# A GNN and mixture-of-experts kernel: first experts in groups of 128 slots with second weights held on chip, part rows gathered during routing, 32-bit count halves

## The chip, the cores and the metric

The kernel runs on one core of one Trainium2 chip. The metric is device time in microseconds (us) of one execution; lower is better. The core has TensorE (PE; its weight loads are listed apart as PEld), VectorE (DVE), ScalarE (ACT), GpSimd (POOL) and SyncE (SP), each with a program of its own, which wait for one another at semaphores. SP and POOL issue the DMAs. POOL also issues every indirect DMA, in which a column of 128 row numbers in on-chip memory picks 128 rows of a table in DRAM.

## The reference, cut to what matters

6250 nodes with 256 features, 200,000 edges sorted by target. Two rounds of a graph layer and an expert layer, each added to the rows:

```python
edge_index = jnp.stack([src, dst])
x = x + L0_gnn(layernorm(x), edge_index)          # graph attention, 8 heads
x = x + L0_ffn(layernorm(x))                      # 8 experts, the best 2 of each row, 256 -> 512 -> 256
x = x + L1_gnn(layernorm(x), edge_index)          # two normalized sums over the edges; needs the node degrees
x = x + L1_ffn(layernorm(x))                      # 8 experts, the best 1, with a capacity

# L0_ffn
top_vals, top_idx = top_k(xn @ Wr + br, 2);  w = softmax(top_vals)
for e in range(8):
    h = gelu(xn @ W1[e] + b1[e])
    y += (h @ W2[e] + b2[e]) * w_full[..., e]
```

## The kernel before

The work is done in stages, one after the other, with a barrier of all engines between two of them.

**The attention stage** (lines 1190 to 1540, names `gat_...`). The edges lie in 104 steps of 16 tiles of 128 edges. For each tile POOL issues one indirect gather (line 1262, `gat_rows`), so 1664 in all, into a ring of four steps. ACT takes the source terms out of a landed step, PE turns them, DVE makes running maxima, exponents and messages (line 1407), and PE sums the messages into windows (line 1520), which DVE adds to the rows (line 1430). Beside that, each step counts 16 sources per partition for the node degrees. The source numbers lie in DRAM as two halves (`source_halves`: number divided by 128, and the remainder), made in the stage of the edge lists (lines 690 to 693). SP loads 16 columns of both into `count_halves`. DVE compares them with a row of numbers (line 1344, two instructions per step: `count_onehot_lo`, 16 x 128 elements, and `count_onehot_hi`, 16 x 49), and PE multiplies the two (line 1525). Halves, numbers and results are bfloat16.

**The front of the experts** (lines 1585 to 1780) finishes the attention rows, normalizes them and computes the router's logits. SP also fills `moe_rows_out` in DRAM with zeros here (line 1779, 25 DMAs).

**Routing** (`route`, line 2430) is one chain on DVE: the best two experts of each row, their weights, the place of each row in its expert's groups of `TOK1` = 256 slots, and then 98 pairs of one-hot tiles (lines 2593 and 2594), which PE multiplies (line 2631) into the tables of slots. POOL does nothing in it.

**The first experts** (`experts`, line 2625) run over 56 groups of 256 slots. `staged` writes, for every engine, a loop over groups with two buffers and a lag per part. Per group SP loads both weights and both biases of the group's expert (lines 2675 to 2679, 512 KB for each weight), POOL gathers 2 x 128 rows (line 2693) and scatters 2 x 128 result rows (line 2700). PE has this order: the hidden products of the group before (line 2735; per 128 of the 512 hidden values the stationary tile is `w1s[:, b, c, f:F:FC]`, every fourth column, and 256 slots stream), two turns for the code tables (line 782), four turns of rows (line 2725), then the output products of the group before (line 2745). An f32 product of two 128-row tiles is two records in the trace, a turn is one. ACT applies the gelu (line 2761), DVE writes the turned rows (line 2777) and adds the bias (line 2788). `DenseTables` runs along in the same loop: POOL gathers 128 rows of `gnn_part_rows` per group (line 755; 62 in all, six of them in `rest_rows`), DVE subtracts a number (line 767), PE turns, ACT copies (line 796), SP stores `unit_codes` (line 740), which the stage after needs.

The later stages (lines 1840 to 2260, and `experts` again for the second experts, with 512 slots) keep their code.

## Time and profile before

| | us |
|---|---|
| three runs: median (lowest to highest) | 5124.44 (5123.76 to 5125.2) |
| the profiled execution's own time | 5124.75 |
| its span, first to last instruction | 5122.9 |
| attention stage, 194 to 2354 | 2160 |
| front, 2354 to 2454 | 100 |
| routing, 2454 to 2532 | 78 |
| first experts, 2532 to 3022 | 490 |
| the rest, to the end | 2101 |

"Busy" is the time in which an engine works at something that the profile counts; "idle before" is the time for which an engine stood still before an instruction, with what ended it. "issue" means that nothing the profile shows was waited for. [...]

### The profile page before, as it was taken

The numbers are of one execution on the slowest core, as the hardware profiler recorded it, in microseconds if no ns is written. First come the engines' busy times: TensorE is split into PE (matmuls) and PEld (weight loads), VectorE is DVE, ScalarE is ACT, GpSimd is POOL, SyncE is SP. The second block draws the span as 40 slices with busy tenths as digits, with TensorE's granted clock in tenths as the row PEclk, the third lists the DMA queues.
The fourth block names the chain that finished last, engine by engine and source line by source line (L and its number), as shares of the span: only waits on it lengthen the run. The fifth ranks groups of instructions, "written<-read, shape, count | busy, mean of one in ns | idle before, by whom it ended". The sixth has DMA issues, their size and how long they took to land. (4 is left out here: it accounts for less than half of the span.)

```text
span 5122.9 us, 87171 instructions
## 1 busy us (share of the span) xinstructions
PE 4174.7 (81%) x27202; PEld 3066.2 (60%) x27203; DVE 3459.0 (68%) x7696; ACT 1648.5 (32%) x2854; POOL 2300.1 (45%) x2330
## 2 busy tenths in 40 slices
PE   3477777777777777776699964799999999958998
PEld 2355555555555555555489953466666666557787
DVE  6366766676667667768622237899998999764444
ACT  1233333333333333333122236333333333231211
POOL 1377777777777777774155620000000000024553
PEclk9677777777777777776799986899999999958999
DMA  4766666666666666656167653454545545453432
GB/s 122 188 164 164 168 162 164 163 169 162 163 165 168 162 163 165 167 157 207 63 218 232 233 176 111 87 98 85 97 87 90 93 89 95 85 184 115 136 122 87
DMA packets 978900, 733.38 MB, mean 143 GB/s; under 512 B 735781, under 2 KB 864352, under 8 KB 976628
## 3 DMA queue, kind: packets, MB, share of 16 engines
q1 hardware_dynamic: 863047, 427.75, 32.6%
q0 software_dynamic: 109264, 296.24, 21.0%
q10 hardware_dynamic: 6364, 6.40, 0.4%
q8 instruction: 141, 2.31, 0.2%
q14 instruction: 84, 0.68, 0.0%
HBM read 485.07 MB, written 92.30 MB: 113 GB/s over the span
## 5 line engine op out<-in xcount | busy, mean ns | idle before, releaser
L1262 POOL DMA_INDIRECT gat_rows<-h_rows,gat_sources x1664 | 1621.9, 975 | 509.9 <-issue 478.8
L1520 PE MATMUL gat_sum_ps<-gat_rows,gat_onehot 128*128 128x265 f32 x3328 | 1261.7, 542 | 3.7 <-DVE gat_rows L1407 3.6
L1520 PEld LDWEIGHTS gat_sum_ps<-gat_rows,gat_onehot 128*128 128x128 f32 x3328 | 861.3, 272 | 218.2 <-DVE gat_rows L1407 4.8
L2207 ACT CAST gnn_z<-build_ps 128x392 bf16<-128x392 f32 x992 | 479.7, 485 | 749.4 <-PE build_ps L2222 749.2
L2231 PE MATMUL back_ps<-zb_pieces,gnn_z 128*128 128x384 bf16 x3038 | 634.6, 325 | 0.0
L2253 PE MATMUL front_ps<-x_res_wide,front_rows 128*128 128x448 bf16 x2604 | 618.1, 351 | 0.0
L2148 DVE TENSOR_TENSOR onehot_low<-dense_codes,dense_iota_bf 128x2048 bf16<-128x2048 bf16 x496 | 603.9, 1218 | 2.0 <-PE build_ps L2222 1.9
L2127 POOL DMA_INDIRECT front_rows<-zf_piece_rows,vrow_nodes x62 | 58.8, 948 | 1148.0 <-PE front_ps L2253 1137.9
L1407 DVE TENSOR_TENSOR gat_rows<-gat_rows,gat_numerators_ps 128x1024 f32<-128x1024 f32 x416 | 502.2, 1207 | 0.0
L2222 PEld LDWEIGHTS build_ps<-onehot_high,onehot_low 128*128 128x128 bf16 x7936 | 352.6, 98 | 184.9 <-issue 38.2
L2735 PE MATMUL moe_hidden_ps<-moe_rows_T,moe_w 128*128 128x256 f32 (+1 forms) x1408 | 450.4, 475 | 2.3 <-DMA moe_b<-in_L_ffn_b 1.5
L2761 ACT ACTIVATE moe_hidden<-moe_hidden_ps,moe_b 128x256 f32<-128x256 f32 (+1 forms) x352 | 194.0, 551 | 765.3 <-PE moe_hidden_ps L2735 765.3
L2745 PE MATMUL moe_out_ps<-moe_w,moe_hidden 128*128 128x256 f32 x1920 | 434.8, 384 | 1.1 <-ACT moe_hidden L2761 1.1
L2735 PEld LDWEIGHTS moe_hidden_ps<-moe_rows_T,moe_w 128*128 128x128 f32 x1408 | 377.5, 322 | 65.3 <-issue 4.8
L2222 PE MATMUL build_ps<-onehot_high,onehot_low 128*128 128x49 bf16 x7936 | 373.5, 188 | 44.0 <-DVE onehot_high L2148 41.5
L1430 DVE TENSOR_TENSOR x_res_wide<-x_res_wide,gat_sum_ps 128x265 f32 x832 | 355.7, 428 | 66.9 <-DVE x_res_wide L1430 66.4
L2745 PEld LDWEIGHTS moe_out_ps<-moe_w,moe_hidden 128*128 128x128 f32 x1920 | 360.1, 190 | 63.0 <-issue 13.9
L2231 PEld LDWEIGHTS back_ps<-zb_pieces,gnn_z 128*128 128x128 bf16 x3038 | 263.2, 97 | 150.7 <-issue 1.3
L1280 ACT ACTIVATE gat_numerators_ps<-gat_exponents 128x128 f32<-128x128 f32 x104 | 29.3, 281 | 906.2 <-DVE gat_exponents L1400 759.4
L2160 DVE TENSOR_TENSOR gnn_z<-gnn_z,front_ps 128x448 f32<-128x448 f32 x434 | 267.8, 617 | 74.8 <-PE front_ps L2253 73.3
L1493 PE MATMUL gat_turned_ps<-ident,gat_src_terms 128*128 128x128 f32 x104 | 49.3, 474 | 324.7 <-ACT gat_src_terms L1274 324.7
L2253 PEld LDWEIGHTS front_ps<-x_res_wide,front_rows 128*128 128x128 bf16 x2604 | 222.9, 97 | 139.8 <-issue 0.3
(377 smaller groups left out, 5467.5 us busy)
## 6 DMA issues: line engine op xcount, KB each, us to landing
moe_w<-in_L_ffn_W SPq DMA_DIRECT2D x112, 512.0 KB
gat_targets<-gat_step_targets SPq DMA_DIRECT2D x104, 512.0 KB
moe_w<-in_L_ffn_w SPq DMA_DIRECT2D x32, 1024.0 KB
gat_rows<-h_rows,gat_sources POOLq DMA_INDIRECT x1664
gat_flags<-gat_tile_flags SPq DMA_DIRECT2D x104, 128.0 KB
normal_rows<-moe_xn_all SPq DMA_DIRECT2D x14, 896.0 KB
mid_taken<-moe_rows_out SPq DMA_DIRECT2D x14, 896.0 KB, 7.4
moe_rows_out<-slot_zeros SPq DMA_DIRECT2D x24, 512.0 KB
```

The source lines that it names most:

```text
L1262: pool.indirect_dma_start(out=g[:, b, t, :], out_offset=None, in_=T.h[:, :], in_offset=bass.IndirectOffsetOnAxis(ap=idx[:, b, t:t + 1], ax ...
L1407: dve.tensor_tensor(rows[:, :, :, 0:HD], rows[:, :, :, 0:HD], pW[:, n * PART:(n + 1) * PART, :].unsqueeze(3).to_broadcast([P, PART, H, HD] ...
L1430: dve.tensor_tensor(window(w), window(w), po[:, s % BANKS, 0:W], ALU.add).then_inc(ad, 1)
L1520: last = pe.matmul(po[:, s % BANKS, 0:W], o[:, b, s * SUB + t, :], g[:, b, s * SUB + t, :], start=t == 0, stop=t == SUB - 1)
L2148: last = dve.tensor_tensor(out[:, n, :, :, :], ct[:, k % SLOTS, a, at].rearrange("p (u t) -> p u t", t=HITS).unsqueeze(2) .to_broadcast(sh ...
L2160: dve.tensor_tensor(yfT[:, at:at + CN], yfT[:, at:at + CN], pf[:, n, 0:CN], ALU.add).then_inc(ya, 1)
L2207: nc.scalar.copy(AT[:, k % 2, :, CHUNK * c:CHUNK * (c + 1)], pb[:, c % 2, 0:CHUNK * NT].rearrange("p (u h) -> p h u", u=CHUNK)).then_inc(a ...
L2222: last = pe.matmul(pb[:, c % 2, u * NT:(u + 1) * NT], ol[:, n, i, :, t], oj[:, n, i, :, t], start=True, stop=True)
L2231: ins = pe.matmul(py[:, (k - 1) % 2, 0:3 * P], AT[:, (k - 1) % 2, h, :], zb3[:, h, :, :].rearrange("p s f -> p (s f)"), start=h == 0, stop ...
L2253: ins = pe.matmul(pf[:, bank, 0:CN], zfv[:, first + s, m * P:(m + 1) * P], AV[:, first + s, chunk * CN:(chunk + 1) * CN], start=n == 0, st ...
L2735: last = pe.matmul(ph[:, f % 2, 0:tok], w1s[:, b, c, f:F:FC], xT[:, b, c, :], start=c == 0, stop=c == 1)
L2745: last = pe.matmul(py[:, q % 2, 0:D], hT[:, f, q * P:(q + 1) * P], w2s[:, b, f, :], start=f == 0, stop=f == FC - 1)
```

## The change

1. `TOK1` goes from 256 to 128: 106 groups of 128 slots in place of 56 of 256.
2. `resident_experts` takes the place of `experts` for the first experts. The second weights, their biases and the first biases of all eight experts lie in on-chip memory for the whole stage (`Resident`); they are loaded in the front, behind the loads of the rows, and a group loads its first weights alone. Each engine that needs the expert's number reads four numbers from a table every two groups (`Choice.fetch`). The hidden units of a product are now 128 neighbouring columns of the first weights (`f * P:(f + 1) * P`). Hidden values have two buffers, their PSUM tile four, and the output products come two groups behind. `phased` writes the loops, without the part for the code tables once its 62 turns are done.
3. All 62 gathers of part rows are issued by POOL during routing (`gather_parts`); in the experts DVE writes a bfloat16 copy (two instructions), which PE turns.
4. `src_hi`, `src_lo`, `src_void`, `source_halves` and `count_halves` become f32. The numbers they are compared with and the one-hots stay bfloat16.
5. Only the pad rows of `moe_rows_out` are zeroed.

```diff
-TOK1 = 256
+TOK1 = 128
...
-        hi = k.sb(ctx, "src_hi", [P, BG * BLK], BF16)
-        lo = k.sb(ctx, "src_lo", [P, BG * BLK], BF16)
+        hi = k.sb(ctx, "src_hi", [P, BG * BLK])
+        lo = k.sb(ctx, "src_lo", [P, BG * BLK])
...
+def gather_parts(pool, S, C, T, parts, sem):
+
+    for s in range(S.SUPER):
+        pool.indirect_dma_start(
+            out=parts[:, s, :, :].rearrange("p a e -> p (a e)"), out_offset=None, in_=T.gnn[:, :],
+            in_offset=bass.IndirectOffsetOnAxis(ap=C.vpart[:, s:s + 1], axis=0)).then_inc(sem, 16)
...
-        hl = k.sb(ctx, "count_halves", [P, RING, 2, CH], BF16)
+        hl = k.sb(ctx, "count_halves", [P, RING, 2, CH])
...
-        self.filled = zero_fill(sp, [self.y1[0:2 * self.S.ROWS, :], *self.more], self.zf, self.zs)
+        pads = self.S.ROWS - self.S.N
+        for a in range(2):
+            sp.dma_start(self.y1[a * self.S.ROWS + self.S.N:(a + 1) * self.S.ROWS, :], self.zf[0:pads, :]).then_inc(self.zs, 16)
+        self.filled = 32
+        self.weights.load(sp)
...
+    def load(self, sp):
+        w1, b1, w2, b2 = self.dram
+        sp.dma_start(self.b1[:, :, :], b1.rearrange("e (c p) -> p e c", p=P), allow_slow_non_contiguous=True).then_inc(self.wl, 16)
+        for e in range(self.X):
+            sp.dma_start(self.w2[:, e, :, :], w2[e].rearrange("(c p) d -> p c d", p=P)).then_inc(self.wl, 16)
...
+            def load(i, b, t, first):
+                e = sp.value_load(gtab[0:1, bass.ds(t, 1)], min_val=0, max_val=W.X - 1)
+                if not first:
+                    sp.wait_ge(hp, (t - 1) * FC)
+                    sp.nop(nofuse=True)
+                sp.dma_start(w1s[:, b, :, :], W.dram[0][bass.ds(e, 1), :, :].rearrange("a (c p) f -> p (a c) f", p=P)).then_inc(wl[b], 16)
+            phased(sp, groups, [(0, None, load), (2, S.SUPER, side.store(sp))], 2)
+            side.stored(sp)
...
+            def take(t):
+                if t >= 2:
+                    pool.wait_ge(tp, t - 1)
+                pool.indirect_dma_start(
+                    out=xr[:, t % 2, :], out_offset=None, in_=xn[:, :],
+                    in_offset=bass.IndirectOffsetOnAxis(ap=src_of[:, t:t + 1], axis=0)).then_inc(xl[t % 2], 16)
+
+            def put(t):
+                pool.wait_ge(yc, t + 1)
+                pool.indirect_dma_start(
+                    out=y[:, :], out_offset=bass.IndirectOffsetOnAxis(ap=dst_of[:, t:t + 1], axis=0),
+                    in_=yo[:, t % 2, :], in_offset=None).then_inc(ys[t % 2], 16)
+            for t in range(groups + 4):
+                if t < groups:
+                    take(t)
+                if t >= 4:
+                    put(t - 4)
...
+            def hidden(i, b, t, first):
+                pe.wait_ge(tc, t + 1)
+                pe.wait_ge(wl[b], i * 16 + 16)
+                for f in range(FC):
+                    if not (first and b == 0):
+                        pe.wait_ge(hc, t * FC + (f + 1 - FC))
+                    for c in range(2):
+                        last = pe.matmul(ph[:, f, 0:P], w1s[:, b, c, f * P:(f + 1) * P], xT[:, b, c, :],
+                                         start=c == 0, stop=c == 1)
+                    last.then_inc(hp, 1)
+
+            def outs(i, b, t, first):
+                e = expert.at(2, b)
+                pe.wait_ge(hc, t * FC + FC)
+                if not first:
+                    pe.wait_ge(yc, t - 1)
+                for f in range(FC):
+                    last = pe.matmul(py[:, b, 0:D], hT[:, b, f, :], W.w2[:, bass.ds(e, 1), f, :].rearrange("p a d -> p (a d)"),
+                                     start=f == 0, stop=f == FC - 1)
+                last.then_inc(yp, 1)
+
+            pe.wait_ge(side.ir, 1)
+            pe.wait_ge(W.wl, W.full)
+            phased(pe, groups, [(1, None, hidden), (1, S.SUPER, side.turn(pe)), (0, None, turn), (2, None, outs)], 2, expert.fetch)
...
-        T.halves = k.dram("source_halves", [P, 2, S.BATCH * CH], BF16)
+        T.halves = k.dram("source_halves", [P, 2, S.BATCH * CH])
...
+                if tables is not None:
+                    k.pg = k.sem("unit_part_rows_gathered")
+                    k.parts = k.sb(ctx, "unit_part_rows", [P, S.SUPER, 2, P])
+                route(k, S, C, tag, tok, logits, bias, choices, X, capacity, src_of, dst_of, weight, gtab, final, tables)
```

On PE, in the first experts just ahead of their loop (names as in the profile; `x8` is eight products, `ISA` works on registers), stands before, for one group of 256 slots, behind the turns and output products of the group before:

```order
L2725 MATMUL moe_turn_ps<-ident,moe_rows 128x128 x4
L2745 MATMUL moe_out_ps<-moe_w,moe_hidden 128x256 x8
L2735 MATMUL moe_hidden_ps<-moe_rows_T,moe_w 128x256 x8
L782 MATMUL codes_ps<-ident,part_rows 128x128 x2
L2725 MATMUL moe_turn_ps<-ident,moe_rows 128x128 x4
L2745 MATMUL moe_out_ps<-moe_w,moe_hidden 128x256 x8
```

and now, for one group of 128 slots (the loads of the expert's number stand before every second group):

```order
L2798 TENSOR_LOAD moe_group_expert
L2890 MATMUL moe_hidden_ps<-moe_rows_T,moe_w 128x128 x8
L771 MATMUL codes_ps<-codes_ident,part_codes 128x128 x2
L2880 MATMUL moe_turn_ps<-ident,moe_rows 128x128 x2
L2900 ISA
L2900 MATMUL moe_out_ps<-moe_w,moe_hidden 128x256
L2900 ISA
L2900 MATMUL moe_out_ps<-moe_w,moe_hidden 128x256
L2900 ISA
L2900 MATMUL moe_out_ps<-moe_w,moe_hidden 128x256
L2900 ISA
L2900 MATMUL moe_out_ps<-moe_w,moe_hidden 128x256
```

Eight hidden products stream 128 columns where eight streamed 256, four output products take the place of eight, and a register instruction stands before each of them.

On POOL, at the start of the experts and in routing, before:

```order
L2693 DMA moe_rows<-normal_rows,moe_slot_source 128x256 x4
L755 DMA part_rows<-gnn_part_rows,vrow_part 128x256
L2693 DMA moe_rows<-normal_rows,moe_slot_source 128x256 x2
L755 DMA part_rows<-gnn_part_rows,vrow_part 128x256
L755 DMA rest_rows<-gnn_part_rows,vrow_part 128x256 x6
L2700 DMA moe_rows_out<-moe_out_rows,moe_slot_target 26880x256 x2
```

and now (the first row opens routing, the two branches behind the 62 gathers are its closing barrier):

```order
L2601 UNCONDITIONAL_BRANCH
L718 DMA unit_part_rows<-gnn_part_rows,vrow_part 128x256 x62
L2435 UNCONDITIONAL_BRANCH
L2849 UNCONDITIONAL_BRANCH
L2854 DMA moe_rows<-normal_rows,moe_slot_source 128x256 x5
```

The gathers of part rows have left the loop of the experts and stand between two barriers with routing's DVE chain.

## Rows read from the trace of the kernel before

**Rows 1.** Stages: us, busy of PE, PEld, DVE, ACT, POOL, clock, DMA, GB/s.

```profile
194.00:2354.00 2160.00, 1647.72 (x8006) 1186.72 (x8007) 1496.49 (x3851) 704.81 (x729) 1621.94 (x1664) 0.75 0.61 162
2354.00:2454.00 100.00, 64.48 (x298) 58.12 (x296) 75.50 (x174) 46.53 (x155) 39.26 (x9) 0.53 0.68 257
2454.00:2532.00 78.00, 46.55 (x200) 31.47 (x200) 70.73 (x275) 1.53 (x2) 0.00 (x0) 0.76 0.00 1
2532.00:3022.00 490.00, 466.64 (x2140) 422.81 (x2140) 121.25 (x286) 124.96 (x287) 278.04 (x286) 0.97 0.67 220
```

**Rows 2.** Groups by line, attention stage: count, busy, mean ns, idle before.

```profile
L1262 POOL DMA_INDIRECT gat_rows<-h_rows,gat_sources x1664 | 1621.9, 975 | 509.9 <-issue 478.8 <-PE gat_sum_ps L1520 27.7 <-DMA gat_sources<-step_sources 3.4
```

**Rows 3.** Waits in the attention stage: total, times, longest.

```profile
DVE gat_running L1353 <- PE gat_turned_ps L1493: 356.2, 104, 12.6
```

**Rows 4.** Timeline of POOL, one step: start, us, instruction.

```profile
1500.47 1.04 POOL L1262 DMA_INDIRECT gat_rows<-h_rows,gat_sources  x1 [0.30 <-issue]
...
1503.06 1.73 POOL L1262 DMA_INDIRECT gat_rows<-h_rows,gat_sources  x1 [0.30 <-issue]
1505.09 0.95 POOL L1262 DMA_INDIRECT gat_rows<-h_rows,gat_sources  x1 [0.30 <-issue]
```

**Rows 5.** Timeline of DVE, the same stretch.

```profile
1500.40 0.29 DVE L1399 TENSOR_TENSOR gat_exponents<-gat_sums 128x128 f32<-128x128 f32 x1
...
1502.74 1.23 DVE L1344 TENSOR_TENSOR count_onehot_lo<-count_halves,count_iota 128x2048 bf16<-128x2048 bf16 x1 [0.99 <-PE gat_sum_ps L1520]
1503.89 0.56 DVE L1344 TENSOR_TENSOR count_onehot_hi<-count_halves,count_iota 128x784 bf16<-128x784 bf16 x1
1507.79 0.42 DVE L1353 TENSOR_TENSOR_SCAN gat_running<-gat_flags,gat_turned_ps 128x128 f32<-128x128 f32 x1 [3.34 <-PE gat_turned_ps L1493]
```

**Rows 6.** Line 1262: ns min/median/max.

```profile
L1262 POOL DMA_INDIRECT gat_rows<-h_rows,gat_sources x1664: 942/946/1925, 195.0 to 2322.3; - x185
```

**Rows 7.** Line 1344.

```profile
L1344 DVE TENSOR_TENSOR count_onehot_lo<-count_halves,count_iota x104: 1224/1226/1227, 228.2 to 2342.7; 128x2048 bf16<-128x2048 bf16 x104
L1344 DVE TENSOR_TENSOR count_onehot_hi<-count_halves,count_iota x104: 557/559/562, 229.3 to 2343.8; 128x784 bf16<-128x784 bf16 x104
```

**Rows 8.** Line 1407, f32 with f32.

```profile
L1407 DVE TENSOR_TENSOR gat_rows<-gat_rows,gat_numerators_ps x416: 1186/1214/1219, 240.2 to 2351.0; 128x1024 f32<-128x1024 f32 x139
```

**Rows 9.** Line 1970, f32 with bfloat16 (`zf_pieces`).

```profile
L1970 DVE TENSOR_TENSOR mid_rest<-gnn_z,zf_pieces x7: 1080/1085/1087, 3066.6 to 3203.2; 128x896 f32<-128x896 f32 x7
```

**Rows 10.** Timeline of PE, one group of the first experts.

```profile
2701.11 4.07 PE L2735 MATMUL moe_hidden_ps<-moe_rows_T,moe_w 128*128 128x256 f32 x16
2705.01 0.38 PE L782 MATMUL codes_ps<-ident,part_rows 128*128 128x128 f32 x2
2705.23 0.60 PE L2725 MATMUL moe_turn_ps<-ident,moe_rows 128*128 128x128 f32 x4
2705.81 3.71 PE L2745 MATMUL moe_out_ps<-moe_w,moe_hidden 128*128 128x256 f32 x16
2709.37 2.88 PE L2735 MATMUL moe_hidden_ps<-moe_rows_T,moe_w 128*128 128x256 f32 x11
```

**Rows 11.** Timeline of the weight loads, first experts.

```profile
2705.12 0.47 PEld L2725 LDWEIGHTS moe_turn_ps<-ident,moe_rows 128*128 128x128 f32 x4
```

**Rows 12.** The same in the front, clock 0.53.

```profile
2445.30 0.93 PEld L1768 LDWEIGHTS moe_po<-w_router,moe_xT 128*128 128x128 f32 x4 [0.87 <-ACT moe_xT L1728]
```

**Rows 13.** DMA issues, first experts: KB each, median us to landing.

```profile
unit_codes<-codes_out SPq DMA_DIRECT2D x49, 64.0 KB, 4.8
```

**Rows 14.** The page, DMA issues.

```profile
mid_taken<-moe_rows_out SPq DMA_DIRECT2D x14, 896.0 KB, 7.4
```

**Rows 15.** DVE, first and last of routing.

```profile
2454.16 0.57 DVE L2498 TENSOR_TENSOR moe_logits<-moe_raw_logits,b_router 128x392 f32<-128x392 f32 x1 [17.00 <-PEq L1658]
...
2531.43 0.22 DVE L2606 TENSOR_SCALAR moe_slot_source<-moe_slot_token 128x112 int32<-128x112 f32 x1
```

**Rows 16.** Groups by line in routing.

```profile
L2594 DVE TENSOR_SCALAR moe_onehot_tile<-iota,moe_slot_tile,moe_token_number 128x112 f32<-128x112 f32 x98 | 33.8, 345 | 0.0
```

288 lines of the change are left out of this document (179 added, 109 removed).

## The prediction

> **What bounds the kernel now.** I read the table of stages first, then in each stage that the change touches who is busy and who waits. Attention takes 2160 us of the span [rows 1]. POOL is busy for 1621.9 us of it in 1664 indirect gathers; of the 509.9 us between them 478.8 are "issue", 0.30 us behind each, and only 27.7 are put down to a buffer that PE frees [rows 2]. 1621.9 + 509.9 = 2132 us, the stage but for its ends: attention is a row of gathers on POOL, 16 x (0.946 + 0.306) = 20.0 us per step at the median gather [rows 6], and 20.5 us by the sums. DVE is busy for 1496 of 2160 us and waits in each step for PE, 356.2 us / 104 = 3.4 us at line 1353 alone [rows 1, 3]. Routing is 78 us in which DVE works and POOL does nothing [rows 1]. In the first experts PE is busy for 467 of 490 us at clock 0.97 [rows 1]: PE sets the pace, 8.26 us per group (2701.11 to 2709.37) [rows 10].
>
> **The 32-bit halves (part 4) are the largest term.** First the duration. With everything bfloat16 a one-hot of 2048 elements takes 1.226 us and one of 784 takes 0.559 us [rows 7]. An f32 sum of 1024 elements takes 1.214 us [rows 8], so f32 goes at half the pace of bfloat16. What counts is one f32 input beside a bfloat16 one, and that form is in the trace: 896 elements in 1.085 us [rows 9]. From 896 to 1024 elements the time grows by 0.129 us, 1.01 ns per element. So 2048 elements come to 1.214 + 1024 x 1.01 = 2.25 us (plus 1.02) and 784 to 0.97 us (plus 0.41). DVE gets 1.43 us per step more, which its 3.4 us of waiting behind these two instructions [rows 3, 5] can hold.
>
> [...]
>
> Then what it does to POOL. One gather per step is stretched: that of 1503.06 takes 1.73 us where the median is 0.946 [rows 4, 6]. It begins while `count_onehot_lo` (1502.74 to 1503.97) runs [rows 5] and ends 0.82 us behind that instruction's end. The gather of 1500.47 takes 1.04 us beside an f32 instruction with two inputs in on-chip memory (line 1399) that ends at 1500.69, and ends 0.82 us behind it as well [rows 4, 5]. So a gather wants something about 0.13 us after its start (0.946 - 0.82), and stands still until such a DVE instruction, bfloat16 or f32, is over. Over the stage the stretch is 1621.9 - 1664 x 0.946 = 47.8 us, 0.46 us per step, nearly all from `count_onehot_lo` [rows 2, 6, 7].
>
> Gathers begin every 1.25 us, so an instruction of 2.25 us must catch one. If it starts at the same phase as now, the caught gather waits for as much longer as the instruction is longer: 1.02 us. Behind it POOL's next gather asks 0.82 + 0.30 + 0.13 = 1.25 us after the end of the first one-hot, when the second (0.97 us) is over, as now. 104 x 1.02 = **106 us**, on POOL's path, which sets the end of the stage. Bounds: at the most favourable phase the wait is 2.25 - 1.25 = 1.0 us, 0.54 more than now: 56 us; at the worst it is 2.25 us: 186 us. I take the equal phase, since the start of the one-hot hangs on PE's sums of gathered rows and those on the same gathers.
>
> [...]
>
> The wider stores of the edge lists and loads of 64 instead of 32 bytes a row lie beside DVE's and POOL's work: 1 us (0 to 4).
>
> **Routing (part 3).** 62 gathers at 0.946 + 0.306 take 77.6 us [rows 2, 6], and the DVE chain beside them 2454.16 to 2531.65, 77.5 us [rows 15]: two equal paths, both ahead of a barrier. DVE's instructions are of the kind that made gathers wait: most read on-chip memory twice, or are one-hots of 0.29 to 0.35 us back to back [rows 16]. A wait of half such an instruction, about 0.13 us, at each gather gives 62 x 0.13 = **+8 us**. Bounds: 0, if they never meet; 62 x 0.35 = 22 us. DVE itself isn't slowed: `count_onehot_lo` takes 1224 to 1227 ns whether or not a gather runs [rows 7]. The slightly wider group tables cost under 1 us. What leaves the experts' loop there was hidden under PE and gives nothing.
>
> **The first experts (parts 1 and 2).** Now, per group of 256 slots [rows 10]: hidden products 3.90 us for 16 records (0.244 each), code turns 0.22 for 2, row turns 4 x 0.11 + 0.14, output products 16 x 0.213 + 0.15. The output products, whose stationary columns are neighbours, are at the pace of their 256 columns; the hidden ones, with every fourth column, are slower by 0.03 us each.
>
> After it, per group of 128: 16 hidden records of 128 columns, 8 output records of 256, 2 row turns, and for 62 groups 2 bfloat16 turns. What 128 f32 columns cost is in the row turns: their 4 weight loads pass in 0.47 us, under 0.12 us each [rows 11]. The loads ahead of the router's products say it at the lower clock: 4 in 0.93 us, at most 0.23 us each, at a granted clock of 0.53 [rows 1, 12]. So loads keep up with 128 columns, which stream in half of 0.213 us: 16 x 0.107 = 1.71, output 8 x 0.213 + 0.15 = 1.86, row turns 0.22 + 0.14, code turns about 0.12 (0.10 to 0.22): 4.05 us, or 3.93 without code turns.
>
> Then the loads. The first weights of group t are asked for when the hidden products of t - 2 are done and needed two group times later, less these products. Their landing isn't listed; 64 KB take 4.8 us from issue and 896 KB 7.4 us [rows 13, 14], by interpolation 512 KB take 6.2 us. Two groups can't be faster than 1.71 + 0.2 + 6.2 = 8.1 us: 4.06 per group, level with PE. I take 4.1. POOL's one gather and one scatter per group are 2 x 1.25 = 2.5 us, under it. The DMAs move 512 + 128 + 128 + 64 KB in 4.1 us, 208 GB/s, against 220 now [rows 1]. The reads of the expert's number fall under the 1.7 us of queued output products. 106 x 4.1 = 435 us against 56 x 8.26 = 463: **-28 us**. Bounds: PE alone, 424 (-39); weights late with 7.4 us, 4.5 per group, 477 (+14). At the start DVE now waits for 1 MB of second biases and for the last part rows before it copies a turned row; PE's first hidden products and all behind them wait for that: +2 us (0 to 6).
>
> The zero fill and the load of the second weights lie in the front, where the chain over PE, ACT and DVE sets the end at 0.68 DMA share [rows 1]: 0.
>
> **Sum.** 106 + 1 + 8 - 28 + 2 = 89 us on the profiled execution's 5124.75 (span 5122.9 and 1.85 around it), which is 0.3 above the median: **5214 us**.
>
> **Rivals.**
> A, the forecast: the longer one-hot holds up one gather per step. For it: rows 4, 5 and 9. 5214, own range 5165 to 5275. 75%.
> B, the other side: the one-hots cost POOL nothing more. Either the form with f32 halves keeps its 1.23 us, or DVE comes to them at a time when the stretch stays 0.46 us per step. Then attention stays at 2160 us and the rest is -17: 5108, faster. It decides as soon as attention grows by less than 17 us, 0.16 us per step. Against it: rows 9, and gathers every 1.25 us. 13%.
> C, DVE's chain takes the whole 1.43 us per step into the step time, because the numerators come late and with them the free buffers: 149 us, 5257. For it: POOL shows 27.7 us under "PE `gat_sum_ps`" [rows 2]; against it: the 3.4 us of slack. 7%.
> D, the experts are bound by the landing of the first weights with A holding, or the change in routing slows DVE too: 5214 + 42 + 14 = 5270. 5%.
>
> **Numbers.** A measurement of this kernel tells about 0.2%, 10 us, from no change. Faster by that: B, 13%, and a hair of A: 0.14. The same: 0.04. Slower: 0.82. The range of 8 in 10 leaves out the lower half of B and the upper end of C and D: 5110 to 5270; the likeliest case's own is 5165 to 5275.
>
> **What would show it.** Right: `count_onehot_lo` at 2.2 to 2.3 us, `count_onehot_hi` near 0.97; gathers of line 1262 at a mean of about 1.04 us, one per step near 2.4 us; attention at about 2266 us; POOL the last to end routing at 86 us; a group of the experts at 4.1 us with hidden products 0.107 us apart. Wrong: one-hots at 1.23 us, or attention under 2180 us; hidden products 0.19 us apart, which would make the experts slower than before by 60 us and more.

## The result, and the profile after

| | us |
|---|---|
| before, in the comparison (4 runs) | 5124.82 (5123.76 to 5125.97) |
| after (4 runs) | 5163.66 (5161.9 to 5165.16) |
| ratio, 95% interval | 1.0076 (1.0058 to 1.0093) |
| forecast | 5214 (5110 to 5270) |

Slower, as forecast, but by 39 us and not by 89. The spans of the two profiled executions differ by 38.6 us (5122.9, 5161.5), and divide so, each stage from its first instruction to that of the next:

| stage | before | after | change | forecast |
|---|---|---|---|---|
| up to the end of attention | 2357.0 | 2452.3 | +95.3 | +107 |
| front | 97.2 | 97.1 | -0.1 | 0 |
| routing | 78.6 | 87.0 | +8.4 | +8 |
| first experts | 491.3 | 430.0 | **-61.3** | -26 |
| the rest | 2098.8 | 2095.1 | -3.7 | 0 |

The stages of the kernel after (the columns are those of [rows 1]):

```profile
194.00:2452.00 2258.00, 1625.68 (x8009) 1148.27 (x8009) 1650.68 (x3854) 704.67 (x729) 1713.38 (x1664) 0.76 0.59 156
2452.00:2549.40 97.40, 63.67 (x294) 57.76 (x294) 74.24 (x172) 46.59 (x156) 38.65 (x9) 0.52 0.57 176
2549.40:2636.30 86.90, 45.76 (x200) 32.25 (x200) 72.39 (x275) 1.48 (x2) 61.77 (x62) 0.76 0.30 94
2636.30:3066.40 430.10, 408.91 (x2880) 380.58 (x2880) 143.19 (x443) 174.25 (x489) 206.12 (x212) 0.98 0.64 206
```

**Attention.** The gathers, whose line is now 1243, against [rows 2]; then the two one-hots against [rows 7] (ns min/median/max):

```profile
L1243 POOL DMA_INDIRECT gat_rows<-h_rows,gat_sources x1664 | 1713.4, 1030 | 510.0 <-issue 479.5 <-PE gat_sum_ps L1501 27.1 <-DMA gat_sources<-step_sources 3.4
```

```profile
L1325 DVE TENSOR_TENSOR count_onehot_lo<-count_halves,count_iota x104: 2291/2293/2366, 228.5 to 2434.7; 128x2048 bf16<-128x2048 f32 x104
L1325 DVE TENSOR_TENSOR count_onehot_hi<-count_halves,count_iota x104: 959/968/971, 230.7 to 2437.0; 128x784 bf16<-128x784 f32 x104
```

POOL is busy for 91.5 us more, and its idle time behind the gathers is the same (510.0 against 509.9). So 1.030 against 0.975 us per gather makes 91.5 of the 95 us. Some 3 more lie behind the last gather, in a tail of 36.3 us against 33.3, with a mean granted clock (TensorE's, as a share of its full speed) of 0.74 against 0.90. One caught gather, on POOL and beside it on DVE:

```profile
1515.78 0.95 POOL L1243 DMA_INDIRECT gat_rows<-h_rows,gat_sources  x1 [0.30 <-issue]
1517.03 2.50 POOL L1243 DMA_INDIRECT gat_rows<-h_rows,gat_sources  x1 [0.30 <-issue]
1519.84 0.94 POOL L1243 DMA_INDIRECT gat_rows<-h_rows,gat_sources  x1 [0.30 <-issue]
```

```profile
1516.43 2.29 DVE L1325 TENSOR_TENSOR count_onehot_lo<-count_halves,count_iota 128x2048 bf16<-128x2048 f32 x1 [0.51 <-PE gat_sum_ps L1501]
1518.64 0.97 DVE L1325 TENSOR_TENSOR count_onehot_hi<-count_halves,count_iota 128x784 bf16<-128x784 f32 x1
```

The gather begins in the one-hot, which ends at 1518.72, and ends at 1519.53, 0.81 us behind it: the pattern of [rows 4, 5] with a longer instruction. It takes 1.55 us longer than the median.

**Routing.** The part gathers (min/median/max), the last of them, the first gather of the experts, and the end of DVE's chain:

```profile
L718 POOL DMA_INDIRECT unit_part_rows<-gnn_part_rows,vrow_part x62: 942/1015/1161, 2550.0 to 2629.4; - x62
```

```profile
2629.41 0.95 POOL L718 DMA_INDIRECT unit_part_rows<-gnn_part_rows,vrow_part  x1 [0.31 <-issue]
2636.36 0.94 POOL L2854 DMA_INDIRECT moe_rows<-normal_rows,moe_slot_source  x1 [6.01 <-POOLq L2435]
```

```profile
2628.32 0.22 DVE L2591 TENSOR_SCALAR moe_slot_source<-moe_slot_token 128x106 int32<-128x106 f32 x1
```

POOL's last gather ends 1.8 us behind DVE's chain, and POOL goes on 6.01 us after it. In the kernel before POOL went on 1.15 us behind DVE's last instruction (2531.65 [rows 15], first gather at 2532.80). DVE's chain itself, 2549.39 to 2628.54, is 1.7 us longer than it was, but it no longer ends last.

**The first experts.** PE in one group of 128 slots without code turns (rows are listed as in [rows 10]; a run of records ends later than the next begins, so starts are compared):

```profile
2950.43 1.95 PE L2890 MATMUL moe_hidden_ps<-moe_rows_T,moe_w 128*128 128x128 f32 x16
2952.22 0.38 PE L2880 MATMUL moe_turn_ps<-ident,moe_rows 128*128 128x128 f32 x2
2952.44 1.89 PE L2900 MATMUL moe_out_ps<-moe_w,moe_hidden 128*128 x8
2954.16 0.27 PE L2890 MATMUL moe_hidden_ps<-moe_rows_T,moe_w 128*128 128x128 f32 x1
```

1.79 + 0.22 + 1.72 = 3.73 us, with nothing between the parts. With code turns it is 3.85, and every fourth of those groups 4.13; the mean over the 105 steps from row turn to row turn (2641.90 to 3045.51) is 3.84.

### The profile page after: what moved, and what is told of

It is laid out like the page before. It is cut to its first block and busy times, and to the rows that moved or that the text cites. A ratio compares the mean times of both kernels' runs of the same rounds, so it can differ in the third digit from the quotient of the medians.

```text
span 5161.5 us, 90934 instructions
## 1 busy us (share of the span) xinstructions
PE 4091.3 (79%) x27942; PEld 2985.3 (58%) x27943; DVE 3637.5 (70%) x7853; ACT 1696.7 (33%) x3055; POOL 2380.6 (46%) x2318
## 5 line engine op out<-in xcount | busy, mean ns | idle before, releaser
L1243 POOL DMA_INDIRECT gat_rows<-h_rows,gat_sources x1664 | 1713.4, 1030 | 510.0 <-issue 479.5
L1501 PE MATMUL gat_sum_ps<-gat_rows,gat_onehot 128*128 128x265 f32 x3328 | 1181.5, 514 | 1.7 <-DVE gat_rows L1388 1.6
L1501 PEld LDWEIGHTS gat_sum_ps<-gat_rows,gat_onehot 128*128 128x128 f32 x3328 | 797.1, 252 | 189.9 <-DVE gat_rows L1388 2.3
L1334 DVE TENSOR_TENSOR_SCAN gat_running<-gat_flags,gat_turned_ps 128x128 f32<-128x128 f32 x104 | 43.8, 421 | 345.0 <-PE gat_turned_ps L1474 345.0
L1325 DVE TENSOR_TENSOR count_onehot_lo<-count_halves,count_iota 128x2048 bf16<-128x2048 f32 x104 | 238.9, 2297 | 64.1 <-PE gat_sum_ps L1501 52.3
L2133 DVE TENSOR_TENSOR onehot_high<-dense_codes,dense_iota_bf 128x784 bf16<-128x784 bf16 x496 | 279.0, 562 | 0.0
L1255 ACT COPY gat_src_terms<-gat_rows 128x128 f32<-128x128 f32 x104 | 43.4, 418 | 662.7 <-DMA gat_rows<-h_rows,gat_sources 662.7
L1474 PEld LDWEIGHTS gat_turned_ps<-ident,gat_src_terms 128*128 128x128 f32 x104 | 18.9, 182 | 398.4 <-ACT gat_src_terms L1255 398.4
```

The costliest lines, as they stand in the source:

```text
L1243: pool.indirect_dma_start(out=g[:, b, t, :], out_offset=None, in_=T.h[:, :], in_offset=bass.IndirectOffsetOnAxis(ap=idx[:, b, t:t + 1], ax ...
L1325: last = dve.tensor_tensor(out[:, :, :, :], hl[:, b, half, :].rearrange("p (u t) -> p u t", t=2).unsqueeze(2).to_broadcast(shape), iob[:, ...
L1501: last = pe.matmul(po[:, s % BANKS, 0:W], o[:, b, s * SUB + t, :], g[:, b, s * SUB + t, :], start=t == 0, stop=t == SUB - 1)
L2133: last = dve.tensor_tensor(out[:, n, :, :, :], ct[:, k % SLOTS, a, at].rearrange("p (u t) -> p u t", t=HITS).unsqueeze(2) .to_broadcast(sh ...
```

## The experiments

Times stand against the kernel before in the same comparison (5125.56, 5126.06, 5127.03 and 5128.07 us in the four of them). B16 is short for "the changed kernel with bfloat16 halves", the first run.

### The halves alone, taken out and put in

e1, the change without its part 4:

```diff
-        hl = k.sb(ctx, "count_halves", [P, RING, 2, CH])
+        hl = k.sb(ctx, "count_halves", [P, RING, 2, CH], BF16)
...                 # and src_hi, src_lo, src_void, source_halves likewise
```

> The changed kernel with the halves of the source numbers in bfloat16 again, all other parts kept. Theory L (the attention stage lost 94.5 us because the one-hots in f32 stand longer in the way of the gathers, and nothing else moved there): the one-hots are back at 1.226 and 0.559 us, attention is back at its length of before, and the time is 5163.7 - 94.5 = 5069 us, 55 us under the kernel before. Rival R (part of the loss comes from another part of the change, such as where buffers or transfers now lie): attention stays 20 us or more above its length of before, 5090 us and more.

Measured: 5075.35 us, ratio 0.9903 (0.9886 to 0.9919).

e2, the kernel before with that part alone (the same lines the other way round):

> The kernel before with the halves of the source numbers in f32 and nothing else changed. Theory L: attention grows by the same 94.5 us, 5124.8 + 94.5 = 5219 us, count_onehot_lo near 2.29 us, the mean gather 1.03 us. Rival R: less than 75 us, under 5200 us.

Measured: 5218.50 us, ratio 1.0182 (1.0165 to 1.0199).

Taken out of the change the halves give back 5163.7 - 5075.4 = 88 us, put into the kernel before they cost 93 us. L holds; the rest of the change by itself is worth 50 us. The gathers in e1 and e2:

```profile
L1243 POOL DMA_INDIRECT gat_rows<-h_rows,gat_sources x1664 | 1623.6, 976 | 510.2 <-issue 479.6 <-PE gat_sum_ps L1501 27.1 <-DMA gat_sources<-step_sources 3.4
```

```profile
L1262 POOL DMA_INDIRECT gat_rows<-h_rows,gat_sources x1664 | 1712.7, 1029 | 510.0 <-issue 477.6 <-PE gat_sum_ps L1520 28.9 <-DMA gat_sources<-step_sources 3.4
```

### The same work in more instructions

e3 (4 and 2 pieces, f32), e4 (2 and 1, bfloat16) and e13 (2 and 1, f32) differ in the counts and the type of the halves (the diff shows e3):

```diff
-                    shape = [P, CH // 2, w, 2]
-                    last = dve.tensor_tensor(out[:, :, :, :], ...
+                    for g in range(4 if half else 2):
+                        n = CH // 2 // (4 if half else 2)
+                        shape = [P, n, w, 2]
+                        last = dve.tensor_tensor(out[:, g * n:(g + 1) * n, :, :], ...
```

> The changed kernel (halves in f32) with the same one-hot elements written by more instructions: count_onehot_lo in 4 of 512 elements, count_onehot_hi in 2 of 392. Theory I (a gather that asks while a DVE instruction with two inputs runs waits for the end of that one instruction only, and gets in before the next): each caught gather waits 0.3 us on the mean instead of 1.2, two or three are caught per step, 0.7 to 0.9 us per step instead of 1.24: 35 to 55 us less, 5110 to 5130 us; no gather near 2.5 us is left, the longest is about 1.6. Rival T (the gather waits until DVE is through with its row of such instructions, or what counts is their sum): no gain, 5164 us or a few us more for the four added instructions, and gathers of 2.5 us and longer.

Measured: 5067.95 us, ratio 0.9889 (0.9873 to 0.9906).

> The changed kernel with bfloat16 halves and count_onehot_lo written by 2 instructions of 1024 elements. Theory I: a caught gather waits 0.3 us on the mean instead of 0.6, so 0.30 us per step instead of 0.46: 10 to 25 us less than with bfloat16 halves alone, 5044 to 5059 us; the longest gathers near 1.6 instead of 1.9 us. Rival T: no gain, 5069 to 5074 us.

Measured: 5047.77 us, ratio 0.9851 (0.9835 to 0.9867).

> The changed kernel with f32 halves (5163.7 us) and count_onehot_lo in 2 instructions of 1024 elements, count_onehot_hi in one as before. In the run with 4 and 2 pieces a gather that started within 0.1 us of a piece's start was not held up, and a gather that a piece had held up asked again just at the start of a later one. Theory I (a gather waits only for an instruction that began before it, and after a release its successor asks 1.25 us later, which here is when the next instruction, 1.19 us later, has just begun): one held gather per step, 0.6 us instead of 1.24: 5070 to 5110 us. Rival P (what made the run with 4 and 2 pieces fast is that its pieces are short, all of them are waited for): the second gather meets the second piece or the 0.97 us of count_onehot_hi, 1.1 us per step and more, 5145 us and over.

Measured: 5163.06 us, ratio 1.0069 (1.0054 to 1.0085).

e3 gained 96 us where I expected 35 to 55, e4 28, as expected, and e13 nothing at all, where theory I had it at 5070 to 5110 us. DVE's work did not shrink in e3, it grew: the one-hots of a step take 3.5 us with their six instructions and 3.2 with two. The gathers shrank, from a mean of 1030 ns to 970, and the longest from 2909 to 1467. First the lines of e3 (a group by line; ns min/median/max), then POOL and DVE in a step of e13:

```profile
L1243 POOL DMA_INDIRECT gat_rows<-h_rows,gat_sources x1664 | 1613.9, 970 | 510.0 <-issue 496.5 <-PE gat_sum_ps L1503 10.1 <-DMA gat_sources<-step_sources 3.4
```

```profile
L1327 DVE TENSOR_TENSOR count_onehot_lo<-count_halves,count_iota x416: 677/685/767, 230.3 to 2340.0; 128x512 bf16<-128x512 f32 x139
```

```profile
1515.98 1.57 POOL L1243 DMA_INDIRECT gat_rows<-h_rows,gat_sources  x1 [0.30 <-issue]
1517.85 1.71 POOL L1243 DMA_INDIRECT gat_rows<-h_rows,gat_sources  x1 [0.30 <-issue]
```

```profile
1515.50 2.36 DVE L1327 TENSOR_TENSOR count_onehot_lo<-count_halves,count_iota 128x1024 bf16<-128x1024 f32 x2 [0.51 <-issue]
1517.77 0.97 DVE L1327 TENSOR_TENSOR count_onehot_hi<-count_halves,count_iota 128x784 bf16<-128x784 f32 x1
```

The first gather is held by the first piece (1515.50 to 1516.72) and ends 0.83 us behind it, though the second piece follows at once: so far theory I. The next gather starts at 1517.85, 0.08 us after the one-hot of 784 elements, and is held to its end. That is what rival P had named as one of its two ways (the second gather meets `count_onehot_hi`), and its time was the right one. I had let a gather go free that starts up to 0.1 us behind an instruction; 0.08 was already too late.

In e3 the pieces start 0.60 us apart. The gather behind a released one starts 0.82 + 0.30 = 1.12 us behind the end of the piece that held the first, which is 1.20 us behind the start of the next piece: level with the one after that, often to 0.01 us, and it goes free. That the two periods agree was luck: the expectation had not counted on it.

So the refined rule, as the traces here show it, is: **a gather is held when it starts after a DVE instruction did that has both inputs in SBUF (the on-chip memory that is not PSUM), to that instruction's end; one that started first is not.** Of the gathers that started over 0.05 us behind the start of such an instruction and over 0.18 us ahead of its end, all were held in the 16 traces: 1464 of 1464 in the one-hots, 406 of 406 in `gat_exponents`, 370 of 370 in two forms of `gat_sums`, and they ended 0.81 to 0.83 us behind it. (Those held by the scan of line 1364, whose inputs all lie in SBUF, ended 0.75 to 0.76 us behind its end in the changed kernel.) The place of the inputs counts. In the changed kernel 349 gathers started within line 1388 (`gat_rows` times `gat_numerators_ps`, 1.21 us, two inputs, one of them in PSUM), and in the kernel before 331 within its line 1407; none of them took over 0.97 us.

How sharp "first" is, twelve of the traces tell at the one-hots. Of the gathers that started up to 0.1 us ahead of one (393) or less than 0.02 us behind its start (153) none was held; of 26 between 0.02 and 0.05 us behind it 5 were; of 142 between 0.05 and 0.1 all. Where the gather got in first at such a close start, the one-hot took up to 0.08 us longer: DVE pays that much at most, and the gather the rest of the instruction.

With the instructions' starts and lengths of each run, and gathers that may start anywhere in their 1.25 us, this rule gives 0.51 us held per step for bfloat16, 1.53 for f32, 0.44 for e3, 0.26 for e4, 1.26 for e13. The traces (busy time less 1664 times the median, over 104 steps) have 0.46, 1.34, 0.38, 0.17 and 1.27: the order is right, and the sizes to 0.2 us. The measured figures in the expectation of e15 below are up to 0.06 higher than this count gives.

### One input in place of two

e9 is B16 and, behind the one-hots:

```diff
+                dve.tensor_reduce(scr[:, :], C.iota[:, 0:P].unsqueeze(1).to_broadcast([P, 11, P]), AX.X, ALU.add)
```

> The changed kernel with bfloat16 halves (5075.4 us) and one more VectorE instruction per step behind the two one-hots: a reduction of 11 x 128 f32 numbers, which has one input, about 1.5 us long; nobody reads its result. It adds to VectorE what the change to f32 added, 1.5 us against 1.43. Theory L (what holds gathers up is a DVE instruction with two inputs, and VectorE's own time is off the path): no more than 10 us, 5065 to 5085 us, no gather longer than with bfloat16 halves alone (1.93 us). Rival C (VectorE's time is on the path, or any DVE instruction holds gathers up): 70 to 156 us more, 5145 us and over.

Measured: 5074.58 us, ratio 0.9898 (0.9883 to 0.9913). DVE's new instruction (a group by line) and the gathers:

```profile
L1330 DVE TENSOR_REDUCE spare_sum<-iota 128x11 f32<-128x1408 f32 x104 | 167.6, 1611 | 0.0
```

```profile
L1244 POOL DMA_INDIRECT gat_rows<-h_rows,gat_sources x1664 | 1622.1, 975 | 510.2 <-issue 479.4 <-PE gat_sum_ps L1503 27.4 <-DMA gat_sources<-step_sources 3.4
```

One step of it, DVE and POOL:

```profile
1259.09 1.61 DVE L1330 TENSOR_REDUCE spare_sum<-iota 128x11 f32<-128x1408 f32 x1
```

```profile
1259.82 0.94 POOL L1244 DMA_INDIRECT gat_rows<-h_rows,gat_sources  x1 [0.30 <-issue]
```

1.61 us per step on DVE cost nothing, where 1.43 us more in instructions with two inputs cost 88. Rival C of the prediction falls. And the reduction did have gathers to hold: in 102 of the 104 steps one starts within it, 0.73 us behind its start on the median, and none takes over 0.95 us. Held as the one-hots hold them, these gathers would have cost about 0.75 us each, an estimate from the rule, 77 us in all. (A twin of this instruction with two inputs in SBUF was not run.)

### The first experts

e6 is B16 with the output products one group earlier (and the expert's number taken to match):

```diff
-            phased(pe, groups, [(1, None, hidden), (1, S.SUPER, side.turn(pe)), (0, None, turn), (2, None, outs)], 2, expert.fetch)
+            phased(pe, groups, [(1, None, hidden), (1, S.SUPER, side.turn(pe)), (0, None, turn), (1, None, outs)], 2, expert.fetch)
```

> The changed kernel with bfloat16 halves (5075.4 us), in which TensorE makes the output products of a group right behind its hidden products, as the kernel before did, instead of one group later. The group of 128 slots takes 3.73 us in the changed kernel's trace without code turns and 3.85 with them; the forecast had 4.05. Theory G (the 0.29 us too much are the two pauses that I carried over from the kernel before, and the later output products are what took them away): pauses of 0.2 to 0.4 us come back ahead of the output products, 106 x 0.29 = 31 us, 5096 to 5118 us. Rival N (a group is only its streaming time, the order of the products costs nothing): 5070 to 5082 us.

Measured: 5144.99 us, ratio 1.0039 (1.0025 to 1.0053). PE in e6:

```profile
2705.66 1.95 PE L2890 MATMUL moe_hidden_ps<-moe_rows_T,moe_w 128*128 128x128 f32 x16
2707.44 0.27 PE L771 MATMUL codes_ps<-codes_ident,part_codes 128*128 128x128 bf16 x2
2707.55 0.39 PE L2880 MATMUL moe_turn_ps<-ident,moe_rows 128*128 128x128 f32 x2
2708.24 1.99 PE L2900 MATMUL moe_out_ps<-moe_w,moe_hidden 128*128 x8 [0.30 <-ACT moe_hidden L2918]
2710.57 1.60 PE L2890 MATMUL moe_hidden_ps<-moe_rows_T,moe_w 128*128 128x128 f32 x12 [0.33 <-issue]
```

The pause ahead of the output products is back (0.69 us from the row turns' start, 0.22 without it), and the first output product takes 0.10 us more. There is more than I expected: a second pause, of 0.33 us, ahead of the hidden products in every fourth group, whose cause no run shows. A group takes 4.42 us, every fourth 4.8 to 5.0. The lag is worth 70 us, 0.66 per group. Rival N falls, and theory G holds in its cause but not in its size: 70 us are twice its 31, and 5145 us lie outside its range.

e7 is B16 with the columns as before:

```diff
-                        last = pe.matmul(ph[:, f, 0:P], w1s[:, b, c, f * P:(f + 1) * P], xT[:, b, c, :],
+                        last = pe.matmul(ph[:, f, 0:P], w1s[:, b, c, f:F:FC], xT[:, b, c, :],
```

> The changed kernel with bfloat16 halves (5075.4 us), with the first weights loaded into TensorE by every fourth column as in the kernel before (and the rows of the second weights and the first biases in the order that goes with it). Theory L (such a load lasts 0.244 us, which in the kernel before just topped the 0.213 us in which 256 columns stream, and 128 columns take 0.112): hidden products 0.244 us apart, 16 x 0.132 x 106 = 224 us more, near 5299 us. Rival A (it adds the same 0.031 us to each product): 16 x 0.031 x 106 = 53 us more, near 5128 us. Rival N: no difference, 5075 us.

Measured: 5262.54 us, ratio 1.0268 (1.0251 to 1.0285). PE in e7:

```profile
2703.29 3.79 PE L2890 MATMUL moe_hidden_ps<-moe_rows_T,moe_w 128*128 128x128 f32 x16
2706.91 0.28 PE L771 MATMUL codes_ps<-codes_ident,part_codes 128*128 128x128 bf16 x2
```

Products 3.62 / 16 = 0.226 us apart on the mean, where columns side by side give 0.112: 187 us, near L (224) and far from A (53). Behind the first, which follows at 0.12 us, they are 0.233 us apart. That is also their distance in the kernel before, where 256 columns stream and not 128; with the columns side by side 256 columns are 0.216 apart (e8, e16). The weight loads (PEld, 2650 to 2950 us) last 0.326 us on the mean in the kernel before and 0.328 in e7, where they last 0.19 with the columns side by side (after, e8, e16). As the distance is the same 0.233 us at both widths, I take it for the pace of the load of every fourth column: it is 0.017 us above the 0.216 of 256 columns and 0.121 above the 0.112 of 128. (The 0.244 of the prediction is the mean of 16 records with two pauses of 0.08 us among them.)

e8 and e16 put the columns side by side in the kernel before; e8 with the biases and second weights in the order that goes with them, e16 with the columns alone:

```diff
-                        last = pe.matmul(ph[:, f % 2, 0:tok], w1s[:, b, c, f:F:FC], xT[:, b, c, :],
+                        last = pe.matmul(ph[:, f % 2, 0:tok], w1s[:, b, c, f * P:(f + 1) * P], xT[:, b, c, :],
...                 # e8 only:
-                sp.dma_start(b1s[:, b, :], b1[bass.ds(e, 1), :].rearrange("a (p c) -> p (a c)", p=P)).then_inc(wl[b], 16)
+                sp.dma_start(b1s[:, b, :], b1[bass.ds(e, 1), :].rearrange("a (c p) -> p (a c)", p=P), allow_slow_non_contiguous=True).then_inc(wl[b], 16)
```

> The kernel before (5124.8 us, groups of 256 slots), with only the columns of a hidden product side by side in the first and second experts (the second weights' rows and the first biases in the order that goes with it). Theories L and A of the run e7 say the same: hidden products 0.213 us apart instead of 0.244, a group of the first experts shorter by 16 x 0.031 = 0.50 us, 56 x 0.50 = 28 us less there; the second experts, whose products have 512 columns, gain nothing if the load is what counts (L), 5097 us, and 16 x 0.031 x 16 = 8 us more if it is a fixed addition (A), 5089 us. Rival M (the transfers become the bound at 7.7 us per group, or the first biases, now read as single numbers, delay the weights): less than 12 us gained, over 5113 us.

Measured: 5122.03 us, ratio 0.9993 (0.9984 to 1.0003): no difference that can be told. PE waits for the expert's loads ten times between 2580 and 3000 us, and never in that stretch of the kernel before (in all, times, longest), in e8:

```profile
PE moe_hidden_ps L2735 <- DMA moe_b<-in_L_ffn_b: 4.7, 10, 1.2
```

> The kernel before with only the columns of a hidden product side by side in the two experts' stages; biases and second weights stay as they are, so a hidden unit gets the bias and the second weight of another and the output is not the reference's. In the run that also changed the order of the biases the shortest groups of the first experts took 7.85 us where 8.17 are usual, many up to 9 us. Theory S (7.85 is what the columns give, the longer groups came from the biases read as single numbers): steady groups of 7.85 us, 56 x 0.32 = 18 us less, 5107 us. Rival T (the transfers can't bring the weights of a group in 7.85 us): groups above 8.0 us on the mean again, less than 8 us gained, over 5117 us.

Measured: 5112.82 us, ratio 0.9970 (0.9958 to 0.9981). Groups of 7.86 us with few exceptions, where the kernel before has 8.17 and e8 anything from 7.86 to 9.4. So the columns are worth 15 us in groups of 256. The groups of the second experts, with 512 columns, gain 0.02 us of 28.6 in both runs, which is L and not A. What eats the gain in e8 is one of two things, as it differs from e16 in both: the first biases, read as single numbers (512 pieces of 4 bytes per group), or the second weights, read in rows of 1024 bytes instead of 4096. In the traces the packets of the second weights fill the same share of the DMA engines' time in both (0.19 in e8, 0.20 in e16, 2600 to 3000 us), and those of the first biases rise from 0.01 to 0.03. That speaks for the biases, but neither was run alone. The change reads both once, in the front.

e12 is the kernel before without its six part rows in one go:

```diff
-        for x in self.rest_at(t):
-            take(self.S.G1 + x, self.vx[:, x, :, :], self.xg)
...
-            for x in self.rest_at(t):
-                turned(2 + x, self.vx[:, x, :, :])
```

> The kernel before (5124.8 us) without the gather, the subtraction, the turns and the copies of the 6 part rows that it makes in one go in its second group of the first experts; their codes are stored from another row, so that part of the output is not the reference's. In the trace of before the row turns of the first groups are 14.64, 9.82 and 8.86 us apart and later ones 8.17. Theory B (TensorE waits there for one copy after the other, 6.5 us, and then runs at the lower clock for a while): 8 to 10 us less, 5115 to 5117 us, and groups of 8.2 to 9 us from the start. Rival W (the first groups are late because their weights are): 14.64 stays above 12 us and the time within 3 us of 5124.8.

Measured: 5116.13 us, ratio 0.9980 (0.9971 to 0.9990). The row turns are now 8.52, 8.02, 8.02 and 10.36 us apart. Theory B: 10 us. In the step of 10.36 PE waits for the expert's loads (0.63 us) and for ACT (0.97), which the theory had not foreseen. What goes was to be seen on PE in the kernel before, at the first groups:

```profile
2556.56 0.38 PE L782 MATMUL codes_ps<-ident,part_rows 128*128 128x128 f32 x2
2557.64 0.41 PE L782 MATMUL codes_ps<-ident,rest_rows 128*128 128x128 f32 x2 [0.70 <-ACT codes_out L796]
2558.60 0.41 PE L782 MATMUL codes_ps<-ident,rest_rows 128*128 128x128 f32 x2 [0.55 <-ACT rest_codes_out L799]
...
2563.39 1.06 PE L2725 MATMUL moe_turn_ps<-ident,moe_rows 128*128 128x128 f32 x4
2564.24 5.17 PE L2745 MATMUL moe_out_ps<-moe_w,moe_hidden 128*128 128x256 f32 x16
```

6.8 us from 2556.56 to the row turns, which other groups reach in 0.22, and then output products at a slower pace: 16 in 5.0 us to the next start, 3.56 in steady groups. The granted clock is 0.5 from 2560.6 to 2567.4, behind the pauses between the copies, and 1.0 on either side; in e12, without them, it stays at 1.0 from 2548.2 on.

### Routing, and the best of both

e11 is B16 with 54 part gathers in routing, and 8 in the experts:

```diff
-                gather_parts(pool, S, C, tables, k.parts, k.pg)
+                gather_parts(pool, S, C, tables, k.parts, k.pg, 0, S.SUPER - LATE)
...
+                if 1 <= t <= 3:
+                    n = S.SUPER - LATE + (0, 3, 5)[t - 1]
+                    gather_parts(pool, S, C, T, side.parts, side.late, n, n + (3, 2, 3)[t - 1])
```

> The changed kernel with bfloat16 halves (5075.4 us), with 54 of the 62 part gathers in routing and the last 8 in the idle time of POOL in the first four groups of the experts. In the changed kernel POOL ends its last part gather 1.9 us after VectorE's chain and starts the experts 6.01 us later, where POOL's wait for the end of routing was 1.1 us behind the chain in the kernel before. Theory E (POOL needs these 6 us after its own last gather, whatever VectorE does): POOL ends 10 us earlier, VectorE's chain is then the last and routing is 6 to 8 us shorter, 5066 to 5070 us. Rival F (the 6 us come at the end of any routing with such gathers, from the later of the two): 1 to 3 us, 5072 to 5075 us.

Measured: 5068.38 us, ratio 0.9885 (0.9870 to 0.9900).

```profile
2526.57 1.01 POOL L721 DMA_INDIRECT unit_part_rows<-gnn_part_rows,vrow_part  x1 [0.30 <-issue]
2537.54 0.94 POOL L2860 DMA_INDIRECT moe_rows<-normal_rows,moe_slot_source  x1 [9.96 <-POOLq L2441]
```

```profile
2536.19 0.22 DVE L2597 TENSOR_SCALAR moe_slot_source<-moe_slot_token 128x106 int32<-128x106 f32 x1
```

The experts begin 1.13 us behind DVE's last instruction again, and routing takes 80.1 us instead of 86.5. Theory E. DVE's chain takes 79.0 us here, 1.5 more than in the kernel before, which is what is left of the loss in routing.

> The changed kernel with bfloat16 halves, count_onehot_lo in 2 instructions, and the last 8 part gathers in the experts. If both gains are what they are alone, 5047.8 us less 6 to 8 us: 5040 to 5042 us, 1.6% under the kernel before; if routing does not get shorter, 5048 us.

Measured: 5047.26 us, ratio 0.9842 (0.9828 to 0.9855). That is 5 us above the 5040 to 5042 expected. Against e9 and e11 of the same comparison (5074.6, 5068.4) the two gains add up but for 6 us; the shorter routing is in the trace (80.2 us), the gathers of this run were a little longer than in e4 (964 against 957 ns).

> The changed kernel with bfloat16 halves, the last 8 part gathers in the experts, and the one-hots in 4 and 2 instructions. The rule (a gather that starts while an instruction with two inputs runs is held until 0.82 us before its own end is 0.82 us behind that instruction's end; one that started first is not held), with the starts and lengths of the instructions of each run and gathers that may begin anywhere, gives 0.51 us per step for bfloat16, 1.53 for f32, 0.26 for bfloat16 with 2 + 1 pieces, 0.44 for f32 with 4 + 2, 1.26 for f32 with 2 + 1; measured were 0.46 to 0.51, 1.24 to 1.35, 0.23, 0.43 and 1.31. For bfloat16 with 4 + 2 it gives 0.13 us: 104 x 0.10 to 0.13 = 10 to 14 us less than 5047 us, 5033 to 5037 us. Rival O (what is won is lost again in more instructions on VectorE, or the shortest pieces hold gathers as long as the longer ones): 5044 us and over.

Measured: 5037.72 us, ratio 0.9827 (0.9814 to 0.9841), and the gathers:

```profile
L1249 POOL DMA_INDIRECT gat_rows<-h_rows,gat_sources x1664 | 1591.0, 956 | 510.0 <-issue 485.9 <-PE gat_sum_ps L1509 20.7 <-DMA gat_sources<-step_sources 3.4
```

The longest gather is 1213 ns (1456 in e4). The time is where the rule had it, but the trace gives the rule less credit: against e4, whose median gather is the same 946 ns, the held time went from 0.17 to 0.16 us per step only, not from 0.26 to 0.13, and of the 10 us against e14 some 5 are that comparison's slower gathers (median 949 ns, 1664 x 0.003). Below 0.2 us per step the rule with evenly spread starts tells nothing. Still this is the fastest version: 1.7% under the kernel before, 2.4% under the change.

## Why the prediction was right and wrong

**The halves: right.** The lengths came out at 2.29 and 0.97 us (forecast 2.25 and 0.97), attention at +95 us for +107; e1 and e2 put 88 to 93 us on this part alone. What I took for the caught gather, "the same phase, 1.02 us more", was wrong in the make and right in the sum. In the kernel before 83 of the 104 `count_onehot_lo` held a gather, for 0.51 us on the mean; now 103 do, for 0.94 to 1.96 us, 1.29 on the mean. With the few that shorter instructions hold, the held time per step went from 0.46 to 1.34 us, and 104 x 0.88 = 91.5 us. Most of the rise is the longer hold; the rest is that a one-hot of 2.29 us can't slip in between two gathers that start 1.25 us apart. The prediction also had every gather ask 0.13 us after its start; the gathers that start just ahead of a one-hot go free (none of 393 was held), so what decides is which of the two starts first. Rival B fell with the rows of line 1325, C with e9. Two inputs in SBUF held the gathers (line 1325, 1.29 us on the mean), one input (e9, none over 0.95 us) or one of two in PSUM (line 1388, none over 0.97 us) did not. DVE, when it came second, was 0.08 us late at most.

**Routing: right in the sum, wrong in the make.** The gathers are stretched by 0.05 us on the mean (61.77 / 62 = 0.996), 3 us and not 8. The other 5 us are POOL's: 6.01 us from its last gather to its next, where 1.1 us of barrier had been enough (e11). I had not priced this; no row before showed a barrier right behind gathers.

**The first experts: the failing step.** The change was to cost 89 us and cost 39. Of the 50 us between them 12 are in attention, 4 in the later stages, and 35 here: -61.3 us where I had -26.

I forecast 4.1 us per group, 435 in all. It was 3.84: (4.10 - 3.84) x 106 = 27 us. Two terms were too large.

- The pair of pauses, "0.14" and "0.15", which I carried over from the group before into both halves of the new one. With them PE's own sum was 4.05 us, 3.93 without code turns; the trace has 3.85 and 3.73. The two pauses are gone (0.29), the hidden products take 0.08 more than my 1.71: 0.20 us per group, 21 us in all. They are waits of the output products for ACT. In the group of [rows 10] the last gelu ends at 2705.68 (the row below, ACT in the kernel before) and the output products start at 2705.81, and the first product behind such a wait takes 0.10 us more than the others. The change puts the output products a group later, and with them behind hidden products that ACT had long finished; in the diff that is one number, `(2, None, outs)`, which I had read and not priced. e6 shows that it is this number: 0.66 us per group, so that the groups of 128 alone, without it, would have eaten all of the rest's gain (5145 against 5075).

```profile
2705.21 0.47 ACT L2761 ACTIVATE moe_hidden<-moe_hidden_ps,moe_b 128x256 f32<-128x256 f32 x1 [0.46 <-PE moe_hidden_ps L2735]
```

- The landing of the first weights, which I had level with PE and for which I took 4.1 in place of PE's mean of 4.00, 11 us in all. The 512 KB issued at 2752.10 had its last packet done at 2755.4, 3.3 us where I interpolated 6.2 (3.0 to 3.7 over the groups), and no hidden product of the steady groups waits for weights. It set nothing.

These make 32; every fourth step of the groups with code turns, at 4.13, and the slower first groups take 5 back. The loads of 128 neighbouring columns do keep up (0.112 us), as I said, and e7 shows what the other half of that sentence is worth: 187 us.

**The start of the experts: not read.** "What leaves the experts' loop there was hidden under PE and gives nothing" was wrong. In the second group of the kernel before the six rows in one go stop PE for 6.6 us, and the groups are 14.64, 9.82 and 8.86 us apart; e12 gives back 10 us. I took one group for all 56, and one of 8.26 us where most take 8.17, which hid half of it: the mean, row turn to row turn (2540.80 to 3000.39, 55 steps), was 8.36, so 56 x 0.10 = 5 us were missing. And for the new waits at the start I had added 2 us: from the first gather to the first row turn it is 5.5 us after and 8.0 before, 4.5 us off.

27 + 5 + 4.5 less 1.7, by which the end of the stage behind the last group has grown, are the 35 us that were missing in the stage (-61.3 for -26). The 3.7 us in the later stages, whose code is the same, I can't name.

## What to carry over

When an instruction on one engine holds up another engine until it ends, its length costs more than its sum: cut it into pieces and place them by the period of the engine that is held (here 96 us came from cutting 2.29 us into four and 0.97 into two, 28 from cutting 1.23 into two, and nothing from cutting 2.29 into two, where the next gather met the instruction behind). When a tile is halved, price the pauses between its parts anew, by who waits for whom in the new order, not by those of the old tile. And read the first groups of a loop beside a steady one: what is done there "once" can cost more than the term that is being argued about.

## What the runs showed of the hardware

- A gather on POOL that started after a one-hot (both inputs in SBUF) was held to that instruction's end: it ended 0.81 to 0.83 us behind it, up to 1.96 us late in the changed kernel. One that started first was not (none of 393), nor one beside a reduction with one input (e9, none over 0.95 us) or beside an instruction with one of two inputs in PSUM (line 1388, none over 0.97 us). The hold is per instruction: a second one that followed at once did not extend it (e13, 0.83 us behind the first piece). DVE, when it was second, was late by 0.08 us at most.
- Products whose f32 weights are loaded by every fourth column were 0.233 us apart, with 128 streamed columns (e7) as with 256 (before). With neighbouring columns they were 0.216 apart with 256 (e8, e16), and 0.112 with 128 (after).
- POOL started its next stage's first gather 6.01 us after its last gather of the stage before, in the changed kernel and in e1, e3, e4, e6, e7, e9 and e13 alike; with its last gather 9 us ahead of the end of DVE's chain it lost nothing (e11: first gather 1.13 us behind that end). Why, no run shows.
- A DVE comparison of f32 with bfloat16 took 1.12 ns per element of a partition (2.293 us for 2048), of bfloat16 alone 0.60.
